# One more group's term rows folded by GpSimd, and a routing step one slot later

## The chip, the cores and the metric

The kernel runs on one core of a Trainium2 chip. The metric is the device time of one execution in microseconds, the median of several. A core has five engines that run their own instruction streams in order and meet only at semaphores: TensorE (PE in the profile, its weight loads PEld), VectorE (DVE), ScalarE (ACT), GpSimd (POOL) and SyncE (SP), which issues most transfers.

## The reference, cut to what matters

The kernel computes one block in float32 for x of shape (16, 128, 256):

```python
x = x + tanh(g_xattn) * xattn(ctx, ctx, layernorm(x))     # heads of 8 channels
x = x + tanh(g_ffn)   * moe(layernorm(x))
# xattn: kv[i,j,h,l] = k[h,i,l]*v[h,j,l]; causal convolution of kv with ssm_kernel[h] over l, plus D[h]*kv;
#        out[j,h,l] = sum over i of (...)[i,j,h,l] * q[h,i,l]
# moe:   probs = softmax(xt @ Wg); e = argmax; gate = its probability
#        pos = place of the token in its expert's queue; kept if pos < 256
#        out = gate * (silu(x W1[e]) * (x W3[e])) W2[e]  +  silu(x sw1) * (x sw3) sw2
```

There are 2048 tokens (16 x 128 rows of 256) and 8 experts, each with a hidden width of 352, and one shared expert that every token passes.

## The kernel before, in words

The sixteen batches go through in four groups of four (`NG`, `GB`). Each group has eight units of two heads (`UNITS`), so there are 32 convolution slots (`CONV`), and further slots behind them. One loop over slots `s` is written out on every engine, and the tables `STEPS`, `THIRD_STEPS` and `LAST_STEPS` say how many slots after its group's units a step runs (`due`). Within a slot each engine has a fixed order.

In slot `s` TensorE convolves unit `s` into one of two banks `z` (`convolve`, lines 1096 and 1099), which waits until VectorE has finished the products of unit `s - 2`. Then it does a matmul group of the shared expert (`feed_forward`, twelve matmuls of line 1187 or line 1211), then what is due, in this order: `logits` (line 1148), `turn_r` (line 1124), `turn_q` (line 1111), `turn_xT` (line 1136), `places` (lines 1159 and 1161). VectorE multiplies `z` by the queries `qr` in six instructions (`products`, line 458) and writes them into `terms`. The sum over i of a head has then eight rows in `terms`. For the first two groups (`FULL_TERMS = 2`) TensorE adds all eight while it transposes: `turn_r(g, k)` issues 4 x 8 = 32 matmuls for each half k, two halves for a group. For groups 2 and 3 GpSimd first adds rows 4 to 7 onto rows 0 to 3 (`fold`, line 611, one instruction for a unit, in the slot after it), and `turn_r` issues 4 x 4 = 16 matmuls a half.

GpSimd also makes the products `kv` of the context two groups of slots ahead (`kv_products`, lines 439 and 442, on even slots), the layer norms' power (`scale_and_bias`, lines 583 and 584), half of the shared weights' split (`split_up`, line 624, slot 12), and the routing's scatters (line 616). In one slot its order is: kv, fold, scale_and_bias, scatter, split_up.

Transposes and small matmuls all write one of two banks `tp`, in the order of the list `TP`: use n waits until the reader of use n - 2 is done (`tp_wait`). Query turns are read by ScalarE (`q_copy`, line 718), everything else by VectorE. The lines that matter:

```python
def turn_r(g, k):
    pe.wait_ge(prods, UNITS * (g + 1))
    if g >= FULL_TERMS:
        pe.wait_ge(folded, UNITS * (g + 1 - FULL_TERMS))
...
for what, step, parts in (("logits", ...), ("r", "turn_r0", ...), ("r", "turn_r1", ...), ("q", "turn_q", (0, 1)),
                          ("xT", "turn_xT", (0, 1)), ("pos", "places", (0,))):
...
if 1 <= s <= CONV and unit(s - 1)[0] >= FULL_TERMS:
    fold(s - 1)
```

Counting from 0, group 1 has units 8 to 15. Its `turn_r` halves stand in slots 17 and 18, its second layer norm's statistics in slot 19 and its scale in slot 20. The first group's logits stand in slot 18 and its places and scatter in slot 20; the query turn of group 3 stands in slot 21, `turn_xT(1)` in slot 22. On ScalarE slot 19's steps are followed by `squares` and `norm2(1)` in slot 20, and by `silu` and `q_copy(3)` in slot 21. On VectorE `choose` (lines 888 to 905) answers the logits, `slot_of_token` (lines 924 to 929) the places, and `gate` (lines 910 to 916) the exponentials; in a slot the statistics come before `choose`.

Of the kernel before, what the change touches and what calls it, by code (L numbers as in the profile page):

```python
# [68 lines left out]
KVRING = 5  # L69
REST_SLOT = 21  # L70
TERMS = 8
FULL_TERMS = 2
HEADS = 24
TROW = HEADS * 64
EXPERT_SPLIT_SLOT = CONV + 12
# [4 lines left out]
STEPS = {  # L80
    "ln1_stats": 1, "ln1_scale": 2, "ln1_apply": 2, "turn_q": 5,
    "turn_r0": 1, "turn_r1": 2, "residual0": 2, "residual1": 3, "ln2_stats": 3, "ln2_scale": 4, "ln2_apply": 4,
    "turn_xT": 6, "tokens_low": 7, "logits": 10, "exp": 10, "places": 12, "gate": 12, "scatter": 12,
}
THIRD_STEPS = {"logits": 1, "exp": 1, "places": 2, "gate": 2, "scatter": 2}
LAST_STEPS = {
# [26 lines left out]
def unit(s):  # L113

    g, i = divmod(s, UNITS)
    return g, (i + 4 * (g % 2)) % UNITS
# [12 lines left out]
def terms_of(g):  # L129

    return TERMS if g < FULL_TERMS else TERMS // 2

# [68 lines left out]
def build(nc, x, ctxt, kpad, skip_d, g_x, g_f, wg, w1, w3, w2, sw1, sw3, sw2, out):  # L201
# [4 lines left out]
    with ExitStack() as ctx:  # L206
# [227 lines left out]
        def kv_products(eng, g, i, first, done):  # L434

            n = 4 - first
            dst, left = kv_planes(g, i, 64 * first, 0, [[64, n], [1, 64]], [[0, n], [1, 64]])
            _, right = kv_planes(g, i, 0, PL * first, [], [[PL, n], [1, 64]])
            eng.tensor_tensor(dst, left, right, ALU.mult)  # L439
            dst, left = kv_planes(g, i, 256, 0, [[1, 32]], [[1, 32]])  # L440
            _, right = kv_planes(g, i, 0, 32, [], [[1, 32]])
            eng.tensor_tensor(dst, left, right, ALU.mult).then_inc(done, 1)
# [127 lines left out]
        def _(pool):  # L570
# [35 lines left out]
            def fold(s):  # L606
                g, u = unit(s)
                pool.wait_ge(prods, s + 1)
                low, high = (view(terms, first_head(g, u) * 64 + i * 4 * TROW, [[TROW, 4], [1, 128]])
                             for i in range(2))  # L610
                pool.tensor_tensor(low, low, high, ALU.add).then_inc(folded, 1)  # L611
# [15 lines left out]
            for s in range(SLOTS):  # L627
                g, i = kv_due(s)
                if g >= 0:
                    kv_place_free(pool, g, i)  # L630
                    kv_products(pool, g, i, 1, kv_pool)
                if 1 <= s <= CONV and unit(s - 1)[0] >= FULL_TERMS:
                    fold(s - 1)
# [442 lines left out]
        def _(pe):  # L1076
# [37 lines left out]
# [4 lines that stand above are left out]
                n = TP_AT[("r", g, k)]  # L1118
# [161 lines left out]
```

## Time and profile before

| | us |
|---|---|
| median of 3 runs | 221.79 (221.16 to 222.21) |
| profiled execution, its own time | 220.91 |
| its span in the trace | 219.1 |
| TensorE busy | 196.5 (90%) |
| TensorE weight loads busy | 178.8 (82%) |
| VectorE busy | 150.1 (68%) |
| GpSimd busy | 125.6 (57%) |
| ScalarE busy | 80.3 (37%) |

The shares are means over the span. The profile lists for each instruction group its line, its busy time, and what ended the idle time before it; the chain of waits follows the work that ended last back from the end. TensorE has 74% of that chain.

### The profile page before, as it was taken

The page shows a single profiled execution, that of the slowest core. Times are in us where ns is not written, and L with a number is a line of the kernel's source. Part 1 is how long each engine was busy: PE and PEld are TensorE (multiplying, and loading weights), DVE is VectorE, ACT ScalarE, POOL GpSimd, SP SyncE. Part 2 cuts the span into 40 slices and gives each one's busy share as a digit, 9 for nine tenths or more (in the row PEclk, how much of TensorE's full clock was granted, in tenths as well). Part 3 has the DMA queues.
Part 4 walks back from the last instruction along what each step waited for, and adds up shares of the span by engine and source line. Part 5 has one row for each costly group of instructions (what it writes and reads, how often), then busy time and mean ns, then how long its engine had stood idle before and what let it go on. Part 6 is the DMA issues. An engine that isn't in the chain of part 4 may idle for free.

```text
span 219.1 us, 3952 instructions
## 1 busy us (share of the span) xinstructions
PE 196.5 (90%) x1344; PEld 178.8 (82%) x1344; DVE 150.1 (68%) x489; ACT 80.3 (37%) x151; POOL 125.6 (57%) x129
## 2 busy tenths in 40 slices
PE   0298899979999989999999998999999999999970
PEld 0267779857999879988989998999999999999950
DVE  4878988599788977679866856453755775567240
ACT  2424413344642471321336238122453245423200
POOL 4697955377744599624583270550075767775751
PEclk9999999999999999999999999999999999999997
DMA  4789995000000010110201899932536689422221
GB/s 123 269 210 353 368 403 213 0 0 4 3 3 0 0 48 3 48 49 3 90 6 51 259 349 344 312 97 94 149 118 195 219 284 295 123 72 88 71 69 48
DMA packets 21925, 29.77 MB, mean 136 GB/s; under 512 B 3262, under 2 KB 19398, under 8 KB 21904
## 3 DMA queue, kind: packets, MB, share of 16 engines
q1 hardware_dynamic: 19248, 22.65, 31.7%
q0 software_dynamic: 2304, 6.05, 8.3%
q10 hardware_dynamic: 352, 0.81, 1.1%
q8 instruction: 11, 0.18, 0.3%
q14 instruction: 10, 0.08, 0.1%
HBM read 21.32 MB, written 8.45 MB: 136 GB/s over the span
## 4 chain that ended last, share of the span: by engine, by line
PE 74%; DMA 8%; DVE 5%; ACT 4%; issue 4%; POOL 1%; POOLq 1%; SPq 1%; ACTq 0%; DVEq 0%
PE fb L1187 15%; PE z L1187 13%; PE z L1211 12%; PE tp L1124 10%; PE z L1099 8%; PE fb L1211 6%; PE z L1096 5%; DMA toep<-kskip_scratch 4%; DVE terms L458 3%; DMA kskip_scratch<-kp 3%; PE tp L1222 2%; ACT xrow L688 2%; DMA dcol<-skip_d 1%; PE tp L1136 1%; DVE stats L837 1%
## 5 line engine op out<-in xcount | busy, mean ns | idle before, releaser
L458 DVE TENSOR_TENSOR terms<-z,qr 128x512 f32<-128x512 f32 (+2 forms) x192 | 48.8, 324 | 8.0 <-PE z L1099 8.0
L1099 PE MATMUL z<-kv,toep 128*128 128x288 f32 x128 | 42.5, 414 | 0.0
L439 POOL TENSOR_TENSOR kv<-ct 128x768 f32<-128x768 f32 x15 | 28.1, 1876 | 13.8 <-PE z L1099 9.3
L665 POOL DMA_INDIRECT kv<-out,tok x16 | 22.2, 1390 | 18.5 <-DMA out<-x_sb 13.9
L1187 PE MATMUL fb<-xTh,wh_gu 128*128 128x256 f32 (+1 forms) x104 | 32.3, 311 | 0.2 <-issue 0.2
L1096 PEld LDWEIGHTS z<-kv,toep 128*128 128x128 f32 x128 | 22.7, 195 | 11.2 <-issue 6.4
L1096 PE MATMUL z<-kv,toep 128*128 128x144 f32 x128 | 27.5, 297 | 3.5 <-DVE terms L458 2.1
L1187 PE MATMUL fb<-xTl,wh_gu 128*128 128x256 f32 (+1 forms) x104 | 29.0, 279 | 0.0
L1187 PE MATMUL fb<-xTh,wl_gu 128*128 128x256 f32 (+1 forms) x104 | 29.0, 279 | 0.0
L611 POOL TENSOR_TENSOR terms<-terms 128x512 f32<-128x512 f32 x16 | 20.3, 1286 | 11.3 <-DVE terms L458 11.3
L616 POOL DMA_INDIRECT xd_scratch<-xrow,dest x16 | 16.1, 1004 | 17.4 <-DVE xrow L916 7.3
L1187 PE MATMUL z<-xTh,wh_gu 128*128 128x256 f32 (+1 forms) x88 | 25.8, 293 | 0.0
L1187 PE MATMUL z<-xTl,wh_gu 128*128 128x256 f32 (+1 forms) x88 | 24.5, 278 | 0.0
L1187 PE MATMUL z<-xTh,wl_gu 128*128 128x256 f32 (+1 forms) x88 | 24.4, 278 | 0.0
L676 POOL DMA_INDIRECT out<-kv,tok x16 | 16.1, 1006 | 12.8 <-DVE kv L957 6.7
L1124 PE MATMUL tp<-ident,terms 128*128 128x128 f32 x192 | 23.0, 277 | 0.0
L1124 PEld LDWEIGHTS tp<-ident,terms 128*128 128x128 f32 x192 | 22.2, 193 | 0.3
L1099 PEld LDWEIGHTS z<-kv,toep 128*128 128x128 f32 x128 | 20.5, 195 | 0.0
L1187 PEld LDWEIGHTS fb<-xTh,wh_gu 128*128 128x128 f32 (+1 forms) x104 | 19.3, 185 | 1.3 <-issue 0.6
L1187 PEld LDWEIGHTS fb<-xTh,wl_gu 128*128 128x128 f32 (+1 forms) x104 | 19.3, 186 | 0.7
L755 ACT ACTIVATE sg<-fb 128x256 f32<-128x256 f32 (+1 forms) x26 | 9.8, 377 | 27.4 <-PE fb L1187 24.2
L1187 PEld LDWEIGHTS fb<-xTl,wh_gu 128*128 128x128 f32 (+1 forms) x104 | 19.3, 185 | 0.0
(128 smaller groups left out, 377.3 us busy)
## 6 DMA issues: line engine op xcount, KB each, us to landing
terms<-w SPq DMA_DIRECT2D x16, 352.0 KB, 9.3
ct<-ctxt SPq DMA_DIRECT2D x3, 768.0 KB, 7.7
xd_scratch<-xrow SPq DMA_DIRECT2D x4, 516.0 KB, 9.8
kv<-xd_scratch SPq DMA_DIRECT2D x8, 258.0 KB, 4.2
out<-x_sb SPq DMA_DIRECT2D x8, 256.0 KB
terms<-w SPq DMA_DIRECT2D x8, 256.0 KB, 9.7
x_sb<-x SPq DMA_DIRECT2D x3, 512.0 KB, 6.5
toep<-kskip_scratch SPq DMA_DIRECT2D x3, 512.0 KB, 8.0
```

Source lines behind the costliest of these rows:

```text
L439: eng.tensor_tensor(dst, left, right, ALU.mult)
L458: return eng.tensor_tensor(view(terms, t0 + row * TROW + col, [[64, 2], *td]), view(src, zo, [[512, 2], *zd]), view(qr, q0 + qo, [[CW, 2], ...
L611: pool.tensor_tensor(low, low, high, ALU.add).then_inc(folded, 1)
L616: pool.indirect_dma_start(out=xd, out_offset=bass.IndirectOffsetOnAxis(ap=dest[:, n:n + 1], axis=0), in_=xrow[:, g % 2, b, :], in_offset=N ...
L665: pool.indirect_dma_start(out=bg[:, e % BRING, t, :], out_offset=None, in_=out_rows, in_offset=bass.IndirectOffsetOnAxis(ap=tok[:, e, t:t ...
L676: pool.indirect_dma_start(out=out_rows, out_offset=bass.IndirectOffsetOnAxis(ap=tok[:, e, t:t + 1], axis=0), in_=fin[:, e % 2, t, :], in_o ...
L755: act.activation(sg[0:n, k % SGS, :], bank[0:n, 0:256], ACT.Silu).then_inc(silu_done, 1)
L1096: pe.matmul(view(z[s % 2], k * 512 + GB, [[PL, NPL], [1, GB]]), toep[:, h, P:2 * P], view(kv, o, [[PL, NPL], [1, GB]]), start=True, stop=F ...
L1099: mm = pe.matmul(z[s % 2][:, k, 0:KVH], toep[:, h, 0:P], view(kv, o, [[1, KVH]]), start=False, stop=True, skip_group_check=True)
L1124: mm = pe.matmul(tp[n % 2][:, j * P:(j + 1) * P], src, ident[:, :], is_transpose=True, start=(t == 0), stop=(t == terms_of(g) - 1))
L1187: mm = pe.matmul(bank[0:rows(blk, c), m * 256:(m + 1) * 256], wt[w % 2][:, col:col + rows(blk, c)], xt[:, place, k, first:first + 256], st ...
L1211: mm = pe.matmul(bank[:, t * L:(t + 1) * L], hidden(blk, c)[0:rows(blk, c), t * P:(t + 1) * P], down[0:rows(blk, c), c * L:(c + 1) * L], s ...
```

## The change

`FULL_TERMS` goes from 2 to 1. So GpSimd folds units 8 to 15 too (in its slots 9 to 16), and `turn_r(1, k)` waits for eight folds and issues 16 matmuls a half in place of 32. For groups 0 and 1, the steps logits and exp go from 10 to 11, and places, gate and scatter from 12 to 13: logits in slots 19 and 27 in place of 18 and 26, places, gate and scatter in slots 21 and 29 in place of 20 and 28. The list `TP` and each engine's order follow from these tables.

```diff
-FULL_TERMS = 2
+FULL_TERMS = 1
...
-    "turn_xT": 6, "tokens_low": 7, "logits": 10, "exp": 10, "places": 12, "gate": 12, "scatter": 12,
+    "turn_xT": 6, "tokens_low": 7, "logits": 11, "exp": 11, "places": 13, "gate": 13, "scatter": 13,
```

## Rows read from the trace of the kernel before

**Rows 1.** Stretches: busy time of each engine (instructions), granted clock, DMA share, GB/s
```profile
core 0: us, PE busy (x) PEld busy (x) DVE busy (x) ACT busy (x) POOL busy (x), PEclk, DMA share, GB/s
68.00:80.00 12.00, 11.27 (x77) 10.06 (x76) 10.41 (x45) 6.33 (x13) 8.07 (x9) 1.00 0.06 22
80.00:100.00 20.00, 20.00 (x140) 18.29 (x140) 14.72 (x53) 5.83 (x12) 12.43 (x12) 1.00 0.08 28
```

**Rows 2.** Chain of waits: start, duration in us, engine, tile, line, instructions
```profile
58.24 3.59 PE tp L1124 x32
61.84 0.25 PE z L1096 x2
...
63.30 0.34 PE tp L1148 x4
63.64 3.79 PE tp L1124 x32
...
80.96 1.39 PE fb L1187 x12
...
88.10 1.80 PE tp L1124 x16
...
94.30 1.98 PE tp L1124 x16
...
116.73 3.79 PE tp L1124 x32
```

**Rows 3.** Chain of waits, from group 1's second statistics to its turn
```profile
68.99 1.54 DVE terms L458 x6
...
72.68 1.03 POOL rstd L583
...
77.80 0.50 ACT qr L718
...
78.43 1.07 PE tp L1136 x8
```

**Rows 4.** Timeline of TensorE: a places matmul, a query turn
```profile
70.33 0.39 PE L1161 MATMUL tp<-acc,ones 128*128 128x32 f32 x2
...
73.64 1.22 PE L1111 MATMUL tp<-ident,xn 128*128 128x128 f32 x8
```

**Rows 5.** Timeline of GpSimd, slots 12 to 18
```profile
46.57 1.81 POOL L624 TENSOR_TENSOR wl_gu<-shared_gu,wh_gu 128x768 fp32r<-128x768 f32 x1
48.34 2.55 POOL L439 TENSOR_TENSOR kv<-ct 128x768 f32<-128x768 f32 x1
...
56.29 1.30 POOL L611 TENSOR_TENSOR terms<-terms 128x512 f32<-128x512 f32 x1 [1.39 <-DVE terms L458]
57.54 1.86 POOL L439 TENSOR_TENSOR kv<-ct 128x768 f32<-128x768 f32 x1
...
59.78 1.27 POOL L611 TENSOR_TENSOR terms<-terms 128x512 f32<-128x512 f32 x1
```

**Rows 6.** Timeline of VectorE: its half of the shared weights' split
```profile
46.61 2.59 DVE L981 TENSOR_TENSOR wl_gu<-shared_gu,wh_gu 128x768 fp32r<-128x768 f32 x1
```

**Rows 7.** Timeline of VectorE, the choice and the gate of group 1
```profile
94.66 0.18 DVE L888 TENSOR_REDUCE mx<-tp 128x4 f32<-128x32 f32 x1
...
96.64 0.19 DVE L905 TENSOR_REDUCE mine<-t 128x4 f32<-128x32 f32 x1
...
105.27 0.23 DVE L916 TENSOR_SCALAR xrow<-gp,tg 128x4 f32<-128x4 f32 x1
```

**Rows 8.** Timeline of GpSimd, folds behind the second group's first scatters
```profile
108.72 3.76 POOL L611 TENSOR_TENSOR terms<-terms 128x512 f32<-128x512 f32 x3
```

**Rows 9.** Stretches at the end, columns as in rows 1
```profile
212.00:213.00 1.00, 0.05 (x1) 0.00 (x0) 0.48 (x1) 0.00 (x0) 0.53 (x2) 1.00 0.26 92
...
216.00:217.00 1.00, 0.00 (x0) 0.00 (x0) 0.00 (x0) 0.00 (x0) 0.00 (x0) 0.52 0.00 0
```

**Rows 10.** Timeline of TensorE at the start
```profile
9.53 1.94 PE L1111 MATMUL tp<-ident,xn 128*128 128x128 f32 x8 [9.53 <-ACT xn L688]
...
14.66 0.41 PE L1096 MATMUL z<-kv,toep 128*128 128x144 f32 x2
```

## The prediction

> **What bounds the kernel now.** Read the stretches first. Around the change TensorE is the bound: it is busy 11.27 of 12 us from 68 to 80 and all 20 us from 80 to 100 [rows 1]. Then follow the chain of waits. It lies on TensorE through both halves of group 1's `turn_r`, 3.59 and 3.79 us [rows 2], and then leaves it for eight microseconds: products of unit 19 on VectorE from 68.99, the statistics behind them, GpSimd's power at 72.68, ScalarE's `norm2(1)` and table load, `silu`, the copy of group 3's first query turn at 77.80, and TensorE's `turn_xT(1)` at 78.43, which waits for the bank that this copy frees [rows 3]. TensorE itself idles less than a microsecond there, because it had conv(21), conv(22), two expert groups and a query turn to do meanwhile. From 80 on it is full [rows 1] and I found no wait on a transfer's own time behind it, so what reaches the end is the time at which conv(23) starts, 79.50 (78.43 + 1.07).
>
> **What it removes.** Half of `turn_r(1)`: 32 matmuls. Halves with four terms take 1.80 and 1.98 us, with eight 3.59 and 3.79 [rows 2]: 3.6 us off TensorE, in slots 17 and 18. All eight folds of group 1 come onto GpSimd. If nothing else moved, the profiled 220.91 would become 217.3.
>
> **The folds' price on GpSimd.** A fold is 1.25 us from start to start (56.29 to 57.54), and a kv product with its small one 2.24 (57.54 to 59.78) [rows 5]. Eight folds are 10.0 us. GpSimd has pauses enough up to slot 12; there the folds come into them, and what they push back (a power, a query norm) is needed only microseconds later, so I cost them at nothing; if that cover were gone, one fold ahead of the second statistics' power would cost 1.25. After `split_up` (46.57 to 48.38) it has no pause: fold(12), kv, fold(13), fold(14), kv, fold(15). The first starts at 48.34, while VectorE is in its half of the split, which took 2.59 us in parallel to GpSimd's [rows 6]. The kv product that stood there took 2.55, where others take 1.86 [rows 5]: two operations that both read two operands from SBUF don't run beside each other here. So I give fold(12) 1.25 + 0.7 = 1.95, and get 48.34 + 1.95 + 2.24 + 2 x 1.25 + 2.24 + 1.25 = 58.5 for the end of fold(15). `turn_r(1, 0)` now waits for that, and TensorE comes to it at 58.24 [rows 2]. So it starts at 58.5, 0.3 us late. Bounds: without the collision 57.8, no wait; with a second one 59.2, 0.7 more.
>
> The Trainium skill ("SBUF — State Buffer", section "SBUF: two separate sides") says that GpSimd and VectorE hold a common port pair exclusively, for a whole instruction, when VectorE has two SBUF inputs. By that rule the products (one input in PSUM) are not touched, and this trace agrees, as 2.59 beside 2.55 us in the split show and no slowed product; by a bandwidth share instead, each product would grow.
>
> **TensorE from there.** A convolution slot is 1.46 us (61.84 to 63.30), logits 0.34, an expert group 1.39 to 1.41 [rows 2], the query turn 1.05, places 0.36 [rows 4]. So: 58.5 + 1.80 = 60.3; conv(18) 61.8; second half 63.7 (it no longer waits behind the logits); conv(19) 65.15; logits 65.5; conv(20) 66.9; conv(21) 68.4, which needs the products of unit 19 (65.2 + 1.54 = 66.8, in time); expert group 69.8; `turn_q(3)` 70.8.
>
> **What is late next: the places.** They stood in slot 20, ahead of the query turn. In slot 21 they stand behind it, and in the list of bank uses they are the second after the first query half: `places(0)` waits until ScalarE has copied `q(3, 0)`. That copy is behind `norm2(1)` on ScalarE, and so behind the chain of rows 3. This chain starts with conv(19)'s end: products of unit 19 at 65.2 in place of 68.99. The power behind the statistics would follow 3.7 later (72.68 - 68.99) at 68.9, but GpSimd works on end: fold(16), kv(3,1) and fold(17) to 58.5 + 1.25 + 2.24 + 1.25 = 63.25; the power for group 3's first norm with its product (1.03 + 0.2) to 64.5; fold(18) 65.7; kv(3,2) and fold(19) to 65.7 + 2.24 + 1.25 = 69.2. From the power to the freed bank it takes 78.43 - 72.68 = 5.75 [rows 3]: 74.9. `choose(0)`, now behind the statistics, writes the exponentials' input at about 69.1, before ScalarE's `norm2` can start at 70.4, and costs the chain nothing; without that cover the exponentials would stand ahead of it, with no more than the 1.05 between 69.1 and 70.15, when the norm's scale is there.
>
> So TensorE stands from 70.8 to 74.9. Queued behind the waiting matmul are conv(22) and its expert group, 2.9 us of work that used to fill just this wait. Then places 75.3, conv(22) 76.7, expert group 78.1, `turn_xT(1)` with no wait 79.0 to 79.1. Conv(23) starts at 79.05 in place of 79.50: **0.45 us gained of 3.6**. The bank for the other half of `turn_xT` is free by then: VectorE reads the places at 75.4, behind the `silu` product.
>
> **Group 1's routing.** In slots 26 to 29 no query turn is due, so nothing stalls: `places(1)` waits for a residual's read that is long past. On VectorE the choice (94.66 to 96.83, 2.2 us) comes behind the statistics of slot 27, and the places and gate behind unit 29's products (1.54) and one expert product (0.35). The gate, done at 105.50 [rows 7], is done at 105.50 - 0.45 + 2.2 + 1.54 + 0.35 = 109.1. The folds behind the two scatters began 3.22 after it (108.72) [rows 7, 8], so three folds end at 109.1 + 3.22 + 3 x 1.25 = 116.1. `turn_r(3)` needs them at 116.73 - 0.45 = 116.3 [rows 2]. I cost this at nothing, with 0.2 us of cover; bounds 0 and 1.2 (one fold more ahead of it).
>
> **The sum.** -3.6 (matmuls) + 0.3 (fold(15)) + 4.1 (the new stand ahead of the places) - 0.9 (the old one ahead of `turn_xT`: 73.64 + 1.05 + 1.46 + 1.39 = 77.54 to 78.43) - 0.35 (a turn that doesn't start up from a stand, about 0.9 in place of 1.07, and the places' own start-up, which the stand now hides) = -0.45. Profiled time 220.91 - 0.45 = 220.5. The median of the runs shown is 0.88 above the profiled one, so **221.4** is the forecast: no measurable change. What a measurement can tell apart here is 0.5%, 1.1 us.
>
> **Rivals.**
>
> 1. The clock falls in the stand (slower). In the kernel before TensorE idles 0.73 us in all from 68 to 80 [rows 1], and the clock stays at 1.00. After its last matmul, at 212.05, the granted clock stays at 1.00 and falls to one half (2.4 to 1.2 GHz) at the start of the stretch from 216, about 4.0 us later [rows 9]. My stand is 4.1 us. At the start the engine worked slowly from 9.53 to 14.66, the turn of eight taking 1.94 in place of 1.22 [rows 4, 10]: at half rate for 5.1 us, 2.6 us lost. Then 220.9 - 0.45 + 2.6 + 0.88 = 224.0; with conv(22) alone slow (1.46 more), 222.8. It decides as soon as the clock falls inside the stand. Against it: one fall seen, and the forecast stand is at its very edge. The Trainium skill ("TensorE: Matmul & The Clock Gate", "Part 1: The HAM clock gate") says too that an idle TensorE goes back to the lower clock; by it this stand may or may not do so from run to run. Chance 0.20.
>
> 2. The stand is shorter and the matmuls' time comes through. Were the places not held by the query copy (if that copy came 3 us earlier), the whole 3.6 less 0.3 would arrive: 218.5. The order in the list of bank uses speaks against it. A part of it, with no collision at fold(12) and GpSimd free for the power at 68.9, would give another 0.6 to 0.9 us: 220.5. Together 0.14 for faster by over 0.5%.
>
> 3. GpSimd becomes the bound: fold(15) at 59.2 and the folds before `turn_r(3)` 1.2 us late. +0.7 and +1.2: 223.3. For it: only 0.2 us of cover at the second. Against it: 8.07 busy of 12 us around the first [rows 1]. Chance 0.06, two thirds of it over the bound.
>
> **How the numbers follow.** Forecast 0.60, rival 1 0.20, rival 2 0.14, rival 3 0.06. Faster 0.14; same 0.62; slower 0.24. The likeliest case alone spans 220.5 to 222.2 (collision or none, spread of the runs). For 8 in 10 I add the parts of rival 2 below and most of rival 1 above: 220.2 to 223.8.
>
> **What would show it.** Line 1124 has 160 matmuls, line 611 24 folds. TensorE's waits show about 4 us for the places (line 1159) on ScalarE's line 718, just before 75, and none for line 1136. Fold(15) ends at about 58.5. The stretch from 80 on has TensorE full and 0.4 us early. The granted clock tells rival 1. I am wrong if conv(23) starts before 78.5 or after 80.

## The result, and the profile after

| | us |
|---|---|
| kernel before, median | 221.47 (220.68 to 222.21) |
| changed kernel, median of 4 runs | 224.50 (223.91 to 225.51) |
| ratio | 1.0144, 95% interval 1.0111 to 1.0178 |
| profiled execution of the changed kernel, its time and span | 225.51, 223.8 |
| mean granted clock, profiled executions | 0.993 before, 0.975 after |

The change made the kernel 1.4% slower, outside the range given. It is what the prediction had as its first rival: the clock fell in the stand ahead of the places. Ratios, here and below, are formed from undisturbed executions, so they need not be those of the medians.

On the page of the changed kernel two lines show it best. Each digit of PEclk is the granted clock of one fortieth of the span, in tenths.

```profile
PE 197.3 (88%) x1312; PEld 179.0 (80%) x1312; DVE 151.9 (68%) x489; ACT 80.5 (36%) x151; POOL 135.3 (60%) x137
...
PEclk9999999999999759999999999999999999999996
```

TensorE has 32 matmuls fewer (1312 for 1344, half of `turn_r(1)`) and GpSimd eight instructions and 9.7 us more, as the change says. Two slices in the middle of the kernel, at 73 to 84 us, have a reduced clock; before there was none.

Some of the waits of TensorE from 26 to 145 us in the changed kernel (who waited for whom, us in total, times, longest):

```profile
PE tp L1159 <- ACT qr L718: 4.2, 1, 4.2
PE z L1096 <- DVE terms L458: 2.0, 4, 0.9
PE tp L1136 <- ACT qr L718: 0.8, 1, 0.8
PE tp L1124 <- issue: 0.3, 1, 0.3
```

The first line is the stand that was forecast: the places (line 1159) on the query copy (line 718), 4.2 us. (The 0.8 on line 1136 is the first group's turn, near 50; at `turn_xT(1)` there is no wait any more.) The last is `turn_r(1, 0)` waiting for fold(15): 0.3, also as forecast.

The chain of waits of the changed kernel, which answers to [rows 3]:

```profile
66.83 1.55 DVE terms L458 x6
...
71.08 1.04 POOL rstd L583
...
76.20 0.50 ACT qr L718
...
76.74 0.64 PE tp L1159 x2
77.38 0.43 PE tp L1161 x2
77.80 0.64 PE z L1096 x2
78.44 0.96 PE z L1099 x2
79.40 0.48 PE z L1096 x2
79.88 0.96 PE z L1099 x2
80.84 2.40 PE fb L1187 x12
83.24 0.87 PE tp L1136 x8
```

Read the last eight lines against the rows of before. Places take 1.07 in place of 0.36, conv(22) 3.04 in place of 1.46, the expert group 2.40 in place of 1.40: 3.3 us more for the same instructions (part of the 0.7 on the places is the start-up from a stand). `turn_xT(1)` ends at 84.11, before at 79.50, 4.6 later, and the two profiled executions differ by 4.6. (0.7 of it this execution had lost at its start, ahead of the first fold: `turn_r(0, 0)` begins at 32.21 in place of 31.54. The medians differ by 3.0.)

The stretches around it, columns as in [rows 1]; the granted clock is the number behind POOL's:

```profile
74.00:76.00 2.00, 0.00 (x0) 0.00 (x0) 2.00 (x11) 1.97 (x4) 1.25 (x2) 1.00 0.00 0
76.00:77.00 1.00, 0.26 (x2) 0.26 (x2) 0.55 (x3) 1.00 (x3) 0.14 (x2) 0.54 0.00 0
77.00:80.00 3.00, 3.00 (x11) 2.71 (x12) 1.29 (x8) 0.81 (x2) 0.00 (x0) 0.50 0.03 5
80.00:83.00 3.00, 3.00 (x14) 2.71 (x14) 1.55 (x6) 0.00 (x0) 2.37 (x3) 0.52 0.12 44
83.00:84.00 1.00, 1.00 (x11) 1.00 (x11) 0.30 (x1) 0.72 (x3) 1.00 (x1) 1.00 0.37 132
```

TensorE did nothing from 72.5 to 76.7. The clock fell just behind 76, 3.6 us into the stand, to one half (1.2 GHz), and was full again from about 83.

There is a second loss. In the timeline of VectorE of the changed kernel, behind the statistics of slots 17 and 19:

```profile
62.20 0.47 DVE L842 TENSOR_SCALAR veps<-mv 128x4 f32<-128x4 f32 x1
62.59 1.32 DVE L843 TENSOR_SCALAR mneg<-mv 128x4 f32<-128x4 f32 x1
63.82 0.74 DVE L871 SCALAR_TENSOR_TENSOR x_sb<-tp,tg,x_sb 128x512 f32<-128x512 f32 x1
...
70.14 0.80 DVE L842 TENSOR_SCALAR veps<-mv 128x4 f32<-128x4 f32 x1
```

In the kernel before line 843 never took over 0.164. And GpSimd at the same times (line 442 is the small part of a kv product):

```profile
62.19 0.45 POOL L442 TENSOR_TENSOR kv<-ct 128x128 f32<-128x128 f32 x1
62.61 1.27 POOL L611 TENSOR_TENSOR terms<-terms 128x512 f32<-128x512 f32 x1
...
69.63 1.28 POOL L611 TENSOR_TENSOR terms<-terms 128x512 f32<-128x512 f32 x1
```

An instruction on four numbers a partition, with a single input, ends only when GpSimd's product or fold is over: line 842 at 62.67 and 70.94, line 843 at 63.91. The first two cost 1.5 us together and delay the residual and the products of unit 18 (64.59), and through them everything behind. The third costs at most 0.1, since the power (line 583) stands behind that same fold in GpSimd's order. The prediction held only instructions with two SBUF inputs to be exposed. The Trainium skill ("SBUF — State Buffer", section "SBUF: two separate sides") names a second class, VectorE's operations in a two-port mode; this trace agrees if these are such.

### The profile page after: what moved, and what is told of

The parts are those of the page before. It is cut to its first block, busy times and chain, and to the rows that moved or that the text cites. A ratio compares the mean times of both kernels' runs of the same rounds, so it can differ in the third digit from the quotient of the medians.

```text
span 223.8 us, 3896 instructions
## 1 busy us (share of the span) xinstructions
PE 197.3 (88%) x1312; PEld 179.0 (80%) x1312; DVE 151.9 (68%) x489; ACT 80.5 (36%) x151; POOL 135.3 (60%) x137
## 4 chain that ended last, share of the span: by engine, by line
PE 75%; DVE 6%; ACT 6%; POOL 5%; issue 4%; DMA 1%; POOLq 1%; ACTq 0%; DVEq 0%
PE fb L1187 16%; PE z L1187 13%; PE z L1211 12%; PE z L1099 10%; PE tp L1124 8%; PE fb L1211 6%; PE z L1096 6%; DVE terms L458 3%; POOL kv L439 2%; POOL rstd L583 2%; DVE stats L837 2%; PE tp L1222 2%; ACT xrow L688 1%; ACT xn L688 1%; DMA dcol<-skip_d 1%
## 5 line engine op out<-in xcount | busy, mean ns | idle before, releaser
L1099 PE MATMUL z<-kv,toep 128*128 128x288 f32 x128 | 44.6, 432 | 0.0
L611 POOL TENSOR_TENSOR terms<-terms 128x512 f32<-128x512 f32 x24 | 31.2, 1313 | 15.0 <-DVE terms L458 15.0
L1096 PEld LDWEIGHTS z<-kv,toep 128*128 128x128 f32 x128 | 23.9, 204 | 11.9 <-issue 7.2
L1187 PE MATMUL fb<-xTh,wh_gu 128*128 128x256 f32 (+1 forms) x104 | 33.0, 318 | 0.3 <-issue 0.3
L1096 PE MATMUL z<-kv,toep 128*128 128x144 f32 x128 | 29.0, 311 | 3.4 <-DVE terms L458 2.3
L439 POOL TENSOR_TENSOR kv<-ct 128x768 f32<-128x768 f32 x15 | 27.3, 1819 | 6.3 <-DMA ct<-ctxt 3.5
L1099 PEld LDWEIGHTS z<-kv,toep 128*128 128x128 f32 x128 | 21.6, 204 | 0.0
L1187 PEld LDWEIGHTS fb<-xTh,wh_gu 128*128 128x128 f32 (+1 forms) x104 | 19.9, 191 | 1.5 <-issue 0.7
L1187 PEld LDWEIGHTS fb<-xTh,wl_gu 128*128 128x128 f32 (+1 forms) x104 | 19.9, 191 | 0.8
L1124 PE MATMUL tp<-ident,terms 128*128 128x128 f32 x160 | 19.2, 276 | 0.3 <-issue 0.3
L1124 PEld LDWEIGHTS tp<-ident,terms 128*128 128x128 f32 x160 | 18.7, 192 | 0.9 <-issue 0.5
```

The lines of the kernel that those rows point to most:

```text
L1096: pe.matmul(view(z[s % 2], k * 512 + GB, [[PL, NPL], [1, GB]]), toep[:, h, P:2 * P], view(kv, o, [[PL, NPL], [1, GB]]), start=True, stop=F ...
L1099: mm = pe.matmul(z[s % 2][:, k, 0:KVH], toep[:, h, 0:P], view(kv, o, [[1, KVH]]), start=False, stop=True, skip_group_check=True)
L1124: mm = pe.matmul(tp[n % 2][:, j * P:(j + 1) * P], src, ident[:, :], is_transpose=True, start=(t == 0), stop=(t == terms_of(g) - 1))
L1187: mm = pe.matmul(bank[0:rows(blk, c), m * 256:(m + 1) * 256], wt[w % 2][:, col:col + rows(blk, c)], xt[:, place, k, first:first + 256], st ...
```

## The experiments

All were measured beside the kernel before, in three sittings (e1 to e4, e5 to e8, e9 to e12), 4 to 12 runs each; its medians there were 221.11, 220.99 and 221.11. The changed kernel itself was not run in them, so a comparison with its 224.50 goes across sittings. One kernel's executions also differ in what they lose at the start, ahead of everything that the edits touch: the first `turn_r` begins between 31.3 us (e4, e10) and 33.05 (e1, e7) in the traces, so total times of single traces are not compared below.

| label | what | median (range) | ratio, 95% | longest stand of TensorE |
|---|---|---|---|---|
| e1_folds | folds, old steps | 223.41 (220.96 to 225.04) | 1.0059, 1.0026 to 1.0092 | 2.5 |
| e2_steps | steps, old folds | 226.17 (225.65 to 226.53) | 1.0214, 1.0182 to 1.0246 | 3.7 |
| e3_busy | change, stand filled | 222.21 (221.93 to 223.11) | 1.0042, 1.0023 to 1.0061 | 0.9 |
| e4_places22 | change, places behind conv(22) | 222.04 (220.39 to 223.17) | 1.0020, 0.9989 to 1.0051 | 2.3 |
| e5_scale_first | change, scale ahead of fold | 226.11 (225.62 to 227.41) | 1.0235, 1.0213 to 1.0257 | 3.6 and 2.1 |
| e6_both | e4 with scale ahead of fold | 225.36 (222.97 to 226.07) | 1.0176, 1.0137 to 1.0216 | 2.7 and 2.1 |
| e7_steps_busy | e2, stand filled | 224.36 (223.87 to 225.33) | 1.0147, 1.0130 to 1.0163 | 0.9 |
| e8_folds_scale_first | e1 with scale ahead of fold | 224.78 (223.88 to 225.17) | 1.0174, 1.0158 to 1.0190 | 2.3 and 2.1 |
| e9_kv_late | e4 with later kv products | 219.05 (218.63 to 219.82) | 0.9898, 0.9873 to 0.9922 | 1.7 |
| e10_kv_late_busy | e9, stand filled | 218.71 (218.31 to 219.53) | 0.9890, 0.9864 to 0.9915 | 0.9 |
| e11_after_kv_late | change with later kv products | 223.05 (221.81 to 224.52) | 1.0093, 1.0060 to 1.0126 | 3.6 |
| e12_folds_kv_late | e1 with later kv products | 221.12 (220.65 to 222.28) | 0.9998, 0.9980 to 1.0016 | 2.1 |

(One run of e4, of 516 us, is not in its range.)

**Is it the clock?** e3 fills the stand with matmuls that nobody reads.

```diff
 def places(g):
     n = TP_AT[("pos", g, 0)]
+    if g == 0:
+        bank, before = f_bank(FU_AT[SHARED_AT[22]])
+        pe.wait_ge(f_free, before + 1)
+        for _ in range(34):
+            pe.matmul(bank[:, 0:256], wh_gu[0][:, 0:P], xTh[:, 0, 0, 0:256], start=True, stop=True)
     tp_wait(pe, n)
```

> The changed kernel with 34 extra matmuls of 256 columns (about 4.0 us by 0.118 each) on TensorE between the query turn of group 3 and places(0), into a bank that the next expert group overwrites. The stand is filled, nothing else moves. If the fall of the clock is the loss, the granted clock stays 1.00, places, conv(22) and the expert group take 3.3 us less than in the changed kernel, and the time is 221.2. If the stand itself or the folds are the loss and the clock is only a bystander, it stays at 224.5.

Measured 222.2. TensorE's waits in e3 have 0.3 us left ahead of the places, the granted clock is 1.00 there, and its chain shows the expert group and `turn_xT(1)` at the old pace:

```profile
78.55 1.41 PE fb L1192 x12
79.96 0.87 PE tp L1136 x8
```

Doing more work on TensorE made the kernel 2.3 us faster (2.2 by the ratios, 1.0144 and 1.0042). So the clock is shown to be the larger part of the 3.0 us. What is left, 0.4% (0.9 us), is not the clock's.

**Which half of the change?** e1 is `FULL_TERMS = 1` with the old steps, e2 the new steps with `FULL_TERMS = 2`.

> Only the folds: FULL_TERMS is 1, logits and places stay in slots 18 and 20, with places ahead of the query turn. My theory is that the changed kernel's 3 us come from the stand of 4.2 us ahead of places and the clock that falls in it, and not from the folds. Then the chain through choose, the products of unit 19 and the query copy sets turn_xT(1) as in the kernel before, TensorE's freed 3.6 us become stands of under 3 us each, the clock stays at 1.00 and the time is 221 to 222.5. Rival, GpSimd's ten microseconds of folds are what costs (fold(15) late, VectorE's small instructions locked out by them): 224 or more.

> Only the steps: logits and places one slot later, FULL_TERMS stays 2. By my theory places now stand behind the query copy here too: TensorE reaches them at about 74.1, the copy frees the bank at about 77.9, a stand of 3.8 us with 2.9 us of work queued behind it, so turn_xT(1) ends 2.5 us later than before: 224.0 if the clock stays up in the stand, 227 if it falls. Rival, the folds are what costs and the steps are harmless: 221.5.

e2 is between the two numbers of my theory at 226.2, and its stretches show the clock at 0.50 from 79 to 82 (it fell only when TensorE had resumed at 78.80). The steps alone cost 5.1 us, more than the whole change; the folds on top of them give 1.7 back (226.2 to 224.5). e7 is e2 with 29 such matmuls in the stand:

> The kernel with only the steps moved (folds as before, 226.2 us, a stand of 3.7 us ahead of places) with 29 extra matmuls that fill the stand. The clock stays at 1.00. If the clock was worth about as much there as in the changed kernel (2.3 us), 223.7 is left: the price of the order alone, about 2.5 us over the kernel before. If the order alone costs nothing and the clock was all, 221.2.

Measured 224.4, clock at 1.00: 1.8 us were the clock's, 3.3 are the price of the steps with the clock up. The 2.5 that I had computed is 0.8 short by the medians. In the trace, `turn_r(1, 0)` starts at 59.93 and `turn_xT(1)` ends at 83.94, 24.0 us for 21.25 in the kernel before (58.24 to 79.49): 2.8 us, near the 2.5; where the other 0.5 lies is not shown. Its chain still goes through the query copy (78.94) and then, one after the other, places, conv(22), the expert group and `turn_xT(1)`, so the order behind that wait is what costs; that the logits moved too has no run of its own.

e1 missed its interval of 221 to 222.5: eight of its twelve runs are above, up to 225.0, four at 221.0 to 221.8. Its one trace is of its second slowest run (224.56), which had the clock at 1.00 until the last matmul and had lost 1.7 us at the start against the trace of before. Lines 842 and 843 are held there as in the changed kernel (0.48 and 1.31), and VectorE's choice in slot 18 is stretched by GpSimd: in its timeline of VectorE,

```profile
67.50 1.03 DVE L891 SCALAR_TENSOR_TENSOR t<-sh,prio 128x32 f32<-128x32 f32 x1
...
69.38 1.80 DVE L901 TENSOR_TENSOR acc<-acc,pair 128x8 f32<-128x8 f32 x1
```

where 0.19 and 0.16 are what they take alone. (Line 891 was held in the kernel before too, 1.04 at 65.29; line 901 was not.) The products of unit 19 wait behind it, and TensorE stands 2.5 us for them. What the quicker runs did otherwise stays open: they have no trace, and the mean clock doesn't tell them apart (0.982 and 0.983 in the four fastest, 0.981 to 0.993 in the others).

**Places behind conv(22).** e4 takes the first group's places, gate and scatter to slot 22 and puts them ahead of `turn_xT` there, so that the 2.9 us of work stand ahead of the same wait again.

```diff
+    if step in ("places", "gate", "scatter") and s < 24:
+        return 0 if s == 22 else -1
...
-for step, work in (("turn_q", turn_q), ("turn_xT", turn_xT), ("places", places)):
+for step, work in (("turn_q", turn_q), ("places", places), ("turn_xT", turn_xT)):
```

> The changed kernel with the first group's places, gate and scatter in slot 22, ahead of turn_xT and behind conv(22) and its expert group. The same wait for the query copy has 2.9 us of work ahead of it again. By my theory the longest stand falls to about 2.3 us (conv(22) waits for VectorE's products of unit 20), the clock stays up, conv(23) starts 0.5 to 1 us earlier than in the kernel before: 220.5 to 221. Rival, the chain behind the query copy costs the same wherever places stand: 224.

The best runs, 220.4 to 220.9, are the forecast; the others go up to 223.2. The mean clock tells them apart with one exception: 0.994 to 0.996 for the four fastest, 0.981 to 0.988 for six of the seven slower ones. The profiled execution is one in which it fell. Its stretches:

```profile
72.00:74.00 2.00, 0.00 (x0) 0.00 (x0) 1.93 (x10) 1.98 (x5) 0.00 (x0) 1.00 0.00 0
74.00:75.00 1.00, 0.86 (x4) 0.75 (x5) 1.00 (x3) 1.00 (x1) 0.93 (x1) 0.71 0.00 0
75.00:76.00 1.00, 1.00 (x5) 0.86 (x4) 0.87 (x5) 0.99 (x4) 1.00 (x2) 0.50 0.00 0
```

TensorE's wait was 2.35 us and ended at 74.14; the clock fell when it was at work again. So a stand of 2.35 us can be enough, where I had put the edge at about 4. Here line 842's hold counts in full: conv(22) waits for VectorE's products of unit 20, behind the choice.

**The held port, first attempt.** e5 moves `scale_and_bias` ahead of `fold` in GpSimd's loop.

```diff
-if 1 <= s <= CONV and unit(s - 1)[0] >= FULL_TERMS:
-    fold(s - 1)
 for what in ("ln1", "ln2"):
     ...
+if 1 <= s <= CONV and unit(s - 1)[0] >= FULL_TERMS:
+    fold(s - 1)
```

> The changed kernel with GpSimd's scale_and_bias ahead of the fold in the same slot. In the changed kernel VectorE's two small instructions behind the statistics (lines 842 and 843) took 0.47 and 1.32 us beside fold(17), and 0.80 beside fold(19), in place of 0.16. My theory: the fold held the SBUF port that they want. Then they go back to 0.16 to 0.25 here, the power starts 1.3 us and then 2.0 us earlier in all, the stand ahead of places falls from 4.2 to about 2.7 us, and the runs lie between 220.2 (clock stays up) and 222.5 (it falls). Rival, those instructions were long for another reason, or the chain has no more to give: 224 to 224.5.

> Folds for group 1, the scale ahead of the fold, and the first group's places, gate and scatter in slot 22 ahead of turn_xT. By my theory all three losses are then gone: conv(22) waits under 1 us, the query copy's wait is covered, no clock fall, and the 3.6 us of matmuls come through but for what folds ahead of turn_r(2) and turn_r(3) may take: 217.8 to 219, narrowly spread. Rival, another wait behind takes the gain back: 220.5 or more.

> Only the folds (steps as before), with the scale ahead of the fold. The run with the folds alone lay between 221.0 and 225.0. Without the held port VectorE is 1.2 us earlier at the products of unit 18, choose still stands between them and those of unit 19: 219.5 to 220.5 where the clock stays up, up to 222 where it falls. Rival, the folds alone are slow for GpSimd's own load: unchanged, 223.4.

All three failed: slower by 1.6 (e5), 3.3 (e6) and 1.4 us (e8) than the same without it. The reorder also moves fold(11) behind slot 12's scale and so pushes back `split_up` and everything behind it, where GpSimd has no pause up to fold(15). The waits of TensorE in e5:

```profile
PE tp L1159 <- ACT qr L718: 3.6, 1, 3.6
PE tp L1124 <- DVE terms L458: 2.1, 1, 2.1
```

The second line is `turn_r(1, 0)`, which in truth waits for fold(15): the releaser is inferred, VectorE's products had long been done, and GpSimd's timeline has that fold from 58.53 to 59.8, and TensorE resumes at 59.89. Behind that stand of 2.1 us the clock was down too (behind the same stand in the traces of e6 and e8 it stayed at 1.00; there it fell at the later ones of 2.7 and 2.3 us):

```profile
58.00:60.00 2.00, 0.11 (x1) 0.14 (x2) 2.00 (x10) 0.75 (x3) 2.00 (x4) 1.00 0.02 4
60.00:62.00 2.00, 2.00 (x11) 2.00 (x12) 1.93 (x7) 0.00 (x0) 2.00 (x2) 0.55 0.00 0
```

And line 842 was held all the same, now by a kv product. From e5's timeline of VectorE:

```profile
61.01 1.81 DVE L842 TENSOR_SCALAR veps<-mv 128x4 f32<-128x4 f32 x1
```

and from its timeline of GpSimd:

```profile
60.98 1.80 POOL L439 TENSOR_TENSOR kv<-ct 128x768 f32<-128x768 f32 x1
```

In slot 19, where GpSimd stood idle, the two lines took 0.17 and 0.16. So the attempt was the wrong edit, but it says that GpSimd's kv product holds them as its fold does.

**The held port, second attempt.** The kv products run far ahead of their use: `kv_due` makes them one group, eight slots, ahead (the description of the kernel says two groups). e9 is e4 with the old order of scale and fold, and makes them later, in slots 17, 19, 22, 26 and 27:

```diff
 def kv_due(s):
+    if s >= 14:
+        return {17: (2, 3), 19: (3, 0), 22: (3, 1), 26: (3, 2), 27: (3, 3)}.get(s, (-1, 0))
     g, i = divmod(s, UNITS)
```

> Scale and fold in the old order again; places, gate and scatter of the first group in slot 22 as before in the run of that name; and GpSimd's kv products from (2,3) on later, in slots 17, 19, 22, 26 and 27, so that the folds of units 12 to 15 and VectorE's small instructions behind the statistics have GpSimd's port free. My theory of the remaining loss (GpSimd's queue and its hold on the port): fold(15) is done before TensorE wants it (no wait ahead of line 1124), lines 842 and 843 take 0.2 us, the products of unit 19 start where conv(19) ends, conv(23) starts 2.5 us earlier than in the kernel before: 218.5 where the clock stays up. One stand of 1.9 us ahead of conv(22) is left; if the clock falls in that too, up to 220.5. Rival, the port and the queue are not what costs: 220.4 to 223 as with places in slot 22 alone.

Measured 219.05, with six runs within 1.2 us. `turn_r(1, 0)` waits no more, and line 843's (here 847) durations are those of before (shortest, median, longest in ns):

```profile
L847 DVE TENSOR_SCALAR mneg<-mv x8: 155/161/164, 6.4 to 122.1; 128x4 f32<-128x4 f32 x8
```

Against e4 it is 3.0 us faster by the medians, and 1.8 by the fastest runs. e11 is the same edit on the changed kernel:

> The changed kernel with the later kv products alone; places stay behind the query turn in slot 21. The stand ahead of them is 3.8 us in place of 4.2 and ends 1.9 us earlier. By my theory 222.5 to 223 (2 us under the changed kernel), with the clock fallen in every run. Rival, the order of places alone sets the time: 224.5.

Measured 223.05, 1.5 under the changed kernel (1.1 by the ratios, whose intervals overlap a little), stand 3.6, clock fallen (0.50 in its stretch from 76 to 78); in its trace lines 842 and 843 (here 844 and 845) take 0.17 and 0.16 again. So making room for the folds on GpSimd is worth something over 1 us within the change; order and clock are the rest. e10 adds 14 matmuls ahead of conv(22) to e9:

> The same with 14 extra matmuls (1.7 us) ahead of conv(22), which fill that stand. If its spread comes from the clock, this one is narrow at the lower end, 218 to 219; if the spread comes from elsewhere, it stays.

218.71, not to be told from e9 (the intervals cover each other), and the spread of 1.2 us stays, so it is not the clock's. In e9's trace the clock is at 1.00 behind the stand of 1.7 us, and the mean clock of its six runs (0.989 to 0.993) is that of e10's (0.990 to 0.994): there was nothing to win. Both beat the kernel before by 1.0%. How much of that the folds give is not shown: the later kv products and the moved steps were not run without them.

> The folds alone, steps as in the kernel before, with the later kv products. By my count TensorE has no stand over 1.1 us (ahead of conv(21) and of turn_xT(1)), turn_xT(1) ends 2.1 us earlier than before: 219 to 219.5, narrowly spread, faster than the kernel before without moving any routing step. Rival, choose between the products of units 18 and 19 holds all of it back: 221.

e12 came out at 221.12, equal to the kernel before: the rival. I had counted on choose taking 2.2 us. kv(3,0), which I put in slot 19, ran at the same time and held line 893 (0.62, until 65.7), and the fold behind it (66.05 to 67.3) held line 900 (1.13). So the products of unit 19 began at 69.04, against 68.99 in the kernel before. (This execution had lost 0.7 at its start, so up to 0.7 was gained there; the medians don't show it.)

```profile
66.21 1.13 DVE L900 TENSOR_TENSOR acc<-acc,oh 128x8 f32<-128x8 f32 x1
...
69.04 1.54 DVE L460 TENSOR_TENSOR terms<-z,qr 128x512 f32<-128x512 f32 x6
```

## Why the prediction was wrong

- *Matmuls gone, folds added.* Right: 160 and 24; the halves of `turn_r(1)` take 2.03 and 1.77.
- *Fold(15) at 58.5, TensorE 0.3 late.* Right: 0.34, and fold(12) took 1.99 beside VectorE's split, where 1.95 was put down. That the folds up to slot 12 push back nothing that counts held: the power of slot 12 began at 46.06, or 45.39 without the start's 0.67, for 45.32.
- *The stand.* The mechanism was right, place and cause. That the size is right too (4.2 us for 4.1) is luck: it began and ended late. It ended at 76.74, or 76.07 without the start's 0.67, for 74.9, and began at 71.8 for 70.8, since conv(21) waited 0.5 us for the products of unit 19.
- *"Products of unit 19 at 65.2", "power at 69.2".* This step failed by 1.0 and 1.2 us. VectorE's two small instructions were held by a small kv product and fold(17) for 1.5 us together, so the residual, the products of unit 18 and with them unit 19's came late. Fold(18) waited 0.9 us for those products of unit 18, and kv(3,2), fold(19) and the power stand behind it on GpSimd. The prediction's sentence "two operations that both read two operands from SBUF don't run beside each other here" was too narrow. The trace of before had little to warn of it, since GpSimd had no long instruction at these moments; one row did: line 842 took 0.35 at 13.26, until GpSimd's small kv product (13.14 to 13.59) was over. With this the step's -0.45 becomes about +0.8; e3 measured +0.9 with the clock up.
- *The clock.* This is the step that turned the answer: the sum has the fall at nothing, and the rival that has it was given 0.20 with 2.6 us. It cost 2.3 by e3 against the changed kernel (3.3 in the profiled execution), and all four runs have a mean clock of 0.974 to 0.982 against 0.988 to 0.996 in those of the kernel before (one of 265 us aside). The error is in the chance: a single fall, 4.0 us after the last matmul, was read as an edge. At the end of the kernel that is one sample of when it falls, not the shortest stand that does it. In e4 and e5 it fell with 2.35 and 2.1 us. Against a forecast stand of 4.1 the fall should have been the likeliest case: -0.45 + 2.6 would have given 224.0. The 2.6 itself came near by luck: it was read from the slow matmuls at the start, where the profile's granted clock is 1.00 (12 to 14 us), so that these rows don't show a fall, and the falls seen here lasted 3.4 to 6.8 us.
- *Folds ahead of `turn_r(3)`.* Right: three folds ended at 120.6, the turn began at 121.5, no wait. Rival 3 did not occur there; GpSimd's load came through VectorE's small instructions instead.

## What to carry to other kernels

When an edit moves an instruction past another in an in-order queue, ask what now stands behind its wait: here one small matmul pair, moved behind a transposition, put 2.9 us of ready work behind a copy, and with the clock up the moved steps cost 3.3 us (e7). In this kernel a stand of TensorE of two microseconds or more was not priced by its length alone: count the case in which the work behind it runs at half rate, and if the stand can't be removed, try to fill it (e3: 34 useless matmuls, 2.3 us gained). Before giving GpSimd more tensor work, look at which short VectorE instructions on the critical chain will run beside it, and move GpSimd's work that isn't due yet out of their way (e9).

## What was not expected of the hardware

The clock fell after stands of 2.35 us (e4, in some runs by their mean clock) and 2.1 us (e5), and in both it fell 0.3 us after TensorE had resumed. It did not fall in the traces of e6 and e8 with the same stand of 2.1 us, nor in that of e1 with one of 2.5; with stands of at most 1.7 us (e9) it was not seen to fall. It came back 6.8 us later in the changed kernel (76.1 to 82.9), where it had fallen well inside the stand, and 3.4 us later in e4 (74.4 to 77.8) and in e2 (78.9 to 82.3). Nor does a lower mean clock always go with a longer time: five of e12's twelve runs have 0.981 to 0.983 with times of 220.8 to 222.3 us, the other seven 0.992 to 0.994 with 220.7 to 221.2; only one of the seven has a trace. The Trainium skill ("TensorE: Matmul & The Clock Gate", "Part 1: The HAM clock gate") calls its window free-running, so that the same stand may or may not be hit; the 2.1 us stand, hit in e5 and not in e6 and e8, agrees. What decides it for a given stand stays open.

A one-input VectorE instruction of 128x4 took 1.32, 1.81 and 2.20 us (changed kernel, e5, e6) beside a fold, a kv product, and a kv product with its small one, and 0.16 to 0.17 without them; GpSimd's power (line 583) did not do this to the choice's two-input instructions: in the changed kernel line 891 took 0.19 at 71.36, inside the power from 71.08 to 72.10, and it is the same in the traces of e5, e9 and e11.
